# Five engines' hand-written step lists of a cross-attention loop, in another order

## What is computed

```python
q = (hidden_states @ Wq + bq).reshape(b, s, NH, HD).transpose(0, 2, 1, 3)
k = (encoder_hidden_states @ Wk + bk).reshape(b, se, NKV, HD).transpose(0, 2, 1, 3)
v = (encoder_hidden_states @ Wv + bv).reshape(b, se, NKV, HD).transpose(0, 2, 1, 3)
k = jnp.repeat(k, GROUPS, axis=1)
v = jnp.repeat(v, GROUPS, axis=1)
q = _rmsnorm(q, qn_w)
k = _rmsnorm(k, kn_w)
scores = jnp.einsum('bhsd,bhed->bhse', q, k) * scale
scores = scores + attention_mask[:, None, :, :]
probs = jax.nn.softmax(scores.astype(jnp.float32), axis=-1).astype(q.dtype)
out = jnp.einsum('bhse,bhed->bhsd', probs, v)
```

## Time and profile before

| | |
|---|---|
| median of 3 runs | 4682.44 us (4677.71 to 4683.45) |
| profiled execution | 4708.63 us, span 4706.5 us |
| first attention, the 31 rounds from the first score of batch 0 to that of batch 31 | 2221.92 us |
| granted clock of TensorE, mean of the span | 0.911 |

### The profile page before, as it was taken

How to read it: one execution, slowest core, us unless ns; L and a number is a source line. 1 busy time by engine, 2 the same in 40 slices (tenths; PEclk the granted TensorE clock), 3 DMA queues, 4 the chain that set the end, 5 groups by cost and what they waited for, 6 DMA issues and landing times. The chain is left out here.

```text
span 4706.5 us, 104529 instructions
## 1 busy us (share of the span) xinstructions
PE 3904.1 (83%) x34578; PEld 2973.1 (63%) x34579; DVE 3443.8 (73%) x5403; ACT 2449.9 (52%) x4087; POOL 2778.1 (59%) x2145
## 2 busy tenths in 40 slices
PE   5669999999999999999999735883199999999945
PEld 3437777767767776777777724773167767677734
DVE  4657787877877777878877236445789888888957
ACT  4635555545545555555555114331157777777843
POOL 5577777767767776777773144335635555555632
PEclk8879999999999999999999967996599999999966
DMA  6357777767767677687774547554344444444410
GB/s 242 113 133 148 167 153 160 168 132 162 161 141 163 145 159 150 152 173 150 155 160 103 172 127 215 140 141 126 113 123 130 119 123 125 124 118 129 110 38 25
DMA packets 1236097, 657.45 MB, mean 140 GB/s; under 512 B 1087825, under 2 KB 1162449, under 8 KB 1230654
## 3 DMA queue, kind: packets, MB, share of 16 engines
q1 hardware_dynamic: 1218654, 606.60, 54.8%
q0 software_dynamic: 9216, 22.03, 1.6%
q10 hardware_dynamic: 7760, 22.55, 1.3%
HBM read 187.16 MB, written 142.34 MB: 70 GB/s over the span
## 5 line engine op out<-in xcount | busy, mean ns | idle before, releaser
L2007 POOL TENSOR_TENSOR b_pTl<-b_pe,b_pTh 125x1344 f16<-125x1344 f32 x192 | 538.4, 2804 | 482.8 <-ACT b_pTh L2066 458.4
L111 PE MATMUL a_pa<-a_pTh,a_ch 125*128 125x224 f16 x3072 | 796.5, 259 | 1.9 <-DMA a_pTl<-a_pl 1.9
L113 PE MATMUL a_pa<-a_pTh,a_cl 125*128 125x224 f16 x3072 | 795.5, 259 | 0.0
L112 PE MATMUL a_pa<-a_pTl,a_ch 125*128 125x224 f16 x3072 | 795.4, 259 | 0.0
L826 POOL TENSOR_TENSOR a_ksq<-a_kb 125x512 f32<-125x512 f32 x384 | 474.0, 1234 | 350.9 <-DVE a_kb L759 283.4
L698 ACT ACTIVATE a_pr<-a_pr,a_nmax 112x1500 f32<-112x1500 f32 x256 | 395.7, 1546 | 374.3 <-DVE a_nmax L777 374.2
L843 POOL TENSOR_TENSOR a_kb<-a_kb,a_rk 125x512 f32<-125x512 f32 x384 | 540.4, 1407 | 69.1 <-POOL a_kb L843 34.8
L791 DVE SCALAR_TENSOR_TENSOR a_pl<-a_pr,a_inv,a_ph 112x1500 f16<-112x1500 f32 x256 | 502.3, 1962 | 46.1 <-ACT a_ph L705 45.2
L705 ACT ACTIVATE a_ph<-a_pr,a_inv 112x1500 f16<-112x1500 f32 x256 | 395.5, 1545 | 222.1 <-DVE a_inv L786 222.1
L2112 DVE TENSOR_REDUCE b_mx<-b_ps 112x3 f32<-112x1500 f32 x256 | 439.0, 1715 | 95.3 <-PE b_ps L2189 93.9
L777 DVE CUSTOM_DVE_ANT_0 a_pr<-a_ps,a_mask 112x1500 f32<-112x1500 f32 x256 | 438.8, 1714 | 70.3 <-PE a_ps L113 65.3
(11 more groups left out here) (376 smaller groups left out, 10953.5 us busy)
## 6 DMA issues: line engine op xcount, KB each, us to landing
b_ks<-b_kn SPq DMA_DIRECT2D x768, 93.8 KB
scratch_cT<-a_cT SPq DMA_DIRECT2D x64, 768.0 KB
b_cT<-scratch_cT SPq DMA_DIRECT2D x32, 1536.0 KB
a_ctx<-ctx SPq DMA_DIRECT2D x128, 360.0 KB
scratch_xd<-q_zero ACTq DMA_DIRECT2D x4, 4736.0 KB
scratch_yd<-e_y SPq DMA_DIRECT2D x74, 256.0 KB
scratch_oT<-a_ot SPq DMA_DIRECT2D x16, 896.0 KB, 4.2
m_oT<-scratch_oT SPq DMA_DIRECT2D x16, 896.0 KB
```

What stands on the lines that cost most here:

```text
L111: nc.tensor.matmul(out, a_hi, b_hi, start=start, stop=False)
L112: nc.tensor.matmul(out, a_hi, b_lo, start=False, stop=False)
L113: return nc.tensor.matmul(out, a_lo, b_hi, start=False, stop=stop)
L2007: nc.gpsimd.tensor_tensor(pTl[:, n % 2, :, 0:RP], pe_[:, n % NP], pTh[:, n % 2, :, 0:RP], ALU.subtract).then_inc(s["l_pool"], 1)
```

## The change

It reorders the entries of the five lists of `ORDER0`. No instruction is added or removed, and no buffer, shape or wait condition is edited. On TensorE, `P16` moves from the end of a batch's own round to the head of the next (`P16<`), the early `K` move ahead (`K3` before `P17<`, `K5` before `P19<`), the `P` of the round's middle and end come one to two places later relative to `S` and `R`, and the last entries are `O1 P15 R10 R11`. On GpSimd the four `D`, before in two pairs, stand singly: `D1` after `q7`, `D2` after `q9`, `D3` after `N5`, and `D0` after the next batch's `N1` (written `D0>` at the list's end). On SyncE `c1` follows `l0`, `c2` stands ahead of `l2`, `c3` ahead of `l3`, `x0` follows `l5`, `k0` precedes `l7`, `h7` comes after `l7` and `c0>`, and `x1` and `k1` close the list.

```diff
--- before.py
+++ after.py
@@ -404,19 +404,19 @@
 
 ORDER0 = {
     "tensor": """
-        K0 S0 K1 K2 S1 P17< P18< K3 S2 K4 P19< P20< P21< R0 K5 O2< P22< R1 P23< S3 R2 P0 P1 K6 P2 R3 K7 S4 K8
-        P3 P4 R4 S5 P5 K9 S6 R5 P6 P7 P8 R6 K10 O3< P9 P10 K11 S7 P11 R7 R8 P12 P13 O0 P14 P15 R9 P16 R10 R11
-        O1""",
+        P16< K0 S0 K1 K2 S1 K3 P17< P18< S2 K4 K5 P19< P20< R0 O2< P21< R1 P22< P23< S3 K6 R2 P0 P1 R3 K7 S4
+        K8 P2 P3 R4 S5 P4 K9 R5 P5 S6 P6 R6 K10 P7 O3< P8 P9 K11 R7 S7 P10 R8 P11 P12 O0 R9 P13 P14 O1 P15 R10
+        R11""",
     "scalar": """
-        S0 H0 G2< S1 H1 S2 R0 Z2< H2 R1 D0 D1 G3< R2 S3 R3 H3 D2 D3 S4 R4 H4 G0 S5 R5 H5 S6 R6 Z3< H6 G1 R7 S7
-        R8 Z0 H7 R9 R10 R11 Z1""",
+        S0 H0 G2< S1 S2 H1 R0 H2 R1 G3< D0 D1 Z2< R2 S3 R3 H3 S4 R4 H4 D2 S5 R5 H5 S6 R6 Z3< H6 R7 G0 D3 S7 R8
+        G1 Z0 H7 R9 R10 R11 Z1""",
     "vector": """
-        S0 K1 K2 I0 Q0 S1 L0 G2< K3 I1 S2 K4 Q1 L1 I2 R0 Z2< K5 L2 R1 Q2 S3 G3< R2 K6 I3 R3 K7 L3 S4 K8 Q3 I4
-        R4 S5 L4 G0 K9 I5 S6 R5 Q4 L5 I6 R6 Z3< K10 L6 K11 S7 Q5 G1 R7 I7 R8 Z0 L7 R9 R10 R11 Z1 K0>""",
+        Z1< S0 K1 K2 I0 Q0 S1 L0 K3 I1 S2 K4 G2< K5 I2 Q1 L1 R0 Q2 L2 R1 S3 K6 R2 G3< I3 Z2< R3 K7 L3 S4 K8 Q3
+        I4 R4 S5 L4 K9 I5 R5 S6 Q4 L5 I6 R6 Z3< K10 L6 K11 G0 S7 Q5 R7 I7 Z0 R8 G1 R9 L7 R10 R11 K0>""",
     "gpsimd": """
-        D0 D1 N2 q6 q7 D2 D3 q8 N3 q9 N4 q10 q11 N5 q0> q1> q2> N0> q3> q4> N1> q5>""",
+        N2 q6 q7 D1 q8 N3 q9 D2 N4 q10 q11 N5 D3 q0> q1> q2> N0> q3> q4> q5> N1> D0>""",
     "sync": """
-        h0 l0 h1 l1 h2 l2 c2 c3 x0 h3 l3 c0> k0 c1> h4 l4 h5 l5 o0< x1 q0> h6 l6 h7 k1 l7""",
+        h0 l0 c1 h1 l1 c2 l2 h2 h3 c3 l3 h4 q0 l4 h5 l5 o0< x0 h6 l6 k0 l7 c0> h7 x1 k1""",
 }
 ORDER1 = {
     "tensor": """
```

## The result

| | before | after |
|---|---|---|
| median | 4682.94 us (4 runs, 4677.71 to 4686.72) | 4551.6 us (4 runs, 4550.15 to 4552.53) |
| ratio | | 0.9723, 95% interval 0.9711 to 0.9735 |
| profiled execution, span | 4706.5 us | 4550.2 us |
| 31 rounds of the first attention | 2221.9 us | 2086.7 us |
| first reading of batch 0's scores | 312.8 us | 309.8 us |

The change takes 131 us away, a little more than the 115 forecast. The two spans differ by 156 us, of which 137 lie in the attention. The stages behind it are untouched, but TensorE's matmuls of the experts' stage reach over 442 us in the one profiled execution (2773.6 to 3215.4) and over 425 in the other (2637.1 to 3062.0). The profiled execution before lay 26 us above its median and the one after 0.7, so the medians show little of that part.

What follows compares the result with a forecast made beforehand. TensorE bounds the kernel, floor 65.9 us a round; 0.5 (`R9`) and 0.4 (`P6`, seam) make 66.8, saving 94.6 over 31 rounds, plus 21.7 for clock falls, less 1.4 at the end: -115, median 4568, range 4538 to 4660.

Steps and rivals of the forecast that it cites:

- the likeliest case: The forecast itself, both TensorE waits gone: 4538 to 4605 us, time 4568, chance 0.60.
- the 13 falls of the clock: In 13 of 31 rounds the clock falls after the pause before `R11`; all go, 13 x 1.67 = 21.7 us.
- the loop's returns: TensorE's three waits with no releaser, 13.4 us; claimed to cost the same after the change.
- What bounds: TensorE sets the pace: 65.9 us floor in a 69.85 us round, at most 3.95 to be had.
- The signs that were named: Rounds of 66.4 to 67.2 us, VectorE waiting before `Q5` not `Q4`, nearly no clock falls; wrong if a wait exceeds 1.
- The wait before `K11`: TensorE's 1.54 us wait for VectorE's `R6`, late through `q9` behind `D2 D3`; goes with 1.0 to spare.
- The wait before `R11`: TensorE's 1.83 us wait for the last scaling of `N5`; ends at 65.1 against 65.5, so it goes.
- `R9`: `Q5` waits 1.0 for `q11`, so `R7` is taken out at 61.0 against 60.6: 0.5 us wait with handover.
- The seam: Start of a round, `K0` needing `R10`'s bank: with `P16<` and `K0` as cover, costs nothing to 0.5 us.
- `P6` behind `l3`: TensorE's `P6` wants `l3`, issued at 40.6 behind `c3`, at 45.6: wait between nothing and 1.7 us.
- rival A: The wait moves to `P6`, through SyncE's strictly ordered queue with `l3` behind `c3`: 4605 to 4655 us, chance 0.19.
- The lock between GpSimd and VectorE: GpSimd blocked under VectorE's `L`: eight at about 1.2 us a round, 9.6 in all; without it 0.5 a round better.

Runs made afterwards that it cites:

- e10: Kernel before, with only the `D` of GpSimd and ScalarE spread and SyncE's list as in the change; 4619.7 us, ratio 0.9792.
- e5: Changed kernel with GpSimd's four `D` back in two pairs, and ScalarE's `D2 D3` and SyncE's `c3` moved to match; 4676.84 us, ratio 0.999.
- e3: Kernel before, old order, with the power in GpSimd's `N` left out (output no longer correct); 4523.57 us, ratio 0.9659.
- e6: Changed kernel with the end of TensorE's list as before: `K0` first, `P16` ahead of `R10`, `O1` last; 4553.96 us, ratio 0.9726.
- e2: Changed kernel with `h3` also put behind `c3` in SyncE's list; 4575.76 us, ratio 0.9777.
- e7: Changed kernel with the power in GpSimd's `N` left out (output no longer correct); 4512.72 us.

## Why the prediction was right, step by step

The median is 4551.6 against 4568 forecast, in the range of 4538 to 4660 and in that of the likeliest case. In the 31 rounds the forecast saved 94.6 + 21.7 = 116.3; the traces show 135.2. Outside them the 1.4 us more at the end of the last batch came as forecast (62.8 us from its first scores to the last `a_ot` before, 64.4 after), and the first scores come 3.0 us earlier, which the sum did not have. The forecast for the profiled execution, 4594, was off by 42, since that execution had 26 us above its median before and 0.7 after.

| term | forecast | traces |
|---|---|---|
| clean round, 31 times | 69.85 to 66.8: 94.6 | 69.85 to 66.05: 117.8 |
| the 13 falls of the clock | 21.7 | 21.7, no fall left outside the returns |
| the loop's returns, over six rounds | 0 | 37.9 to 32.5: 5.4 |
| late landings of `l3` | in the 66.8 | -5.9, in four rounds (three more are within the returns') |
| ends of the loop and the rest | 0 | -3.8 |

That the gain at the returns, which was not foreseen, makes up for the late landings is chance.

- **What bounds.** TensorE, with the floor of 65.9: right. A clean round stands 0.15 above it. The count of the rounds was off by one: 13 + 11 + 2 + 6 makes 32, and ten rounds, not eleven, have the pause and no fall.
- **The signs that were named.** The mechanism held: no wait of VectorE before `Q4`, 0.53 before `Q5`, no fall of the clock outside the returns. Two signs did not. Clean rounds are below the 66.4 to 67.2. And the prediction called itself wrong if the longest wait of a round is above 1 us anywhere: in rounds 4, 10, 16 and 22 TensorE waits 1.3 to 1.9 for `a_pTl`, so there the cover of `P6` was misjudged, at a price of 5.9 us.
- **The wait before `K11`.** Named rightly, with GpSimd's backlog behind `D2 D3` as its cause; the new ends of `D1`, `q9` and `D2` (39.3, 46.9, 48.8) came within 0.2 of those worked out (39.5, 47.0, 48.9). e10, e5 and e3 show the cause.
- **The wait before `R11`.** It is gone, and the last of `N5` came 0.5 earlier than the sum had it. e10 adds what the argument did not separate: the spread `D` leave 1.1 of it, TensorE's new places of `R10` and `R11` and VectorE's list take the rest.
- **`R9`.** The 0.5 was the largest mis-sized term. `q11` came at 58.7, not 59.2, so `R7` was taken out 0.1 before `R9` wanted the bank. An error of 0.5 in a chain of 59 us was as large as the wait that was read from it. It is 31 x 0.5 = 15.5 us of the forecast's error.
- **The seam.** The sum gave nothing to 0.5, and it is nothing. e6 shows that the cover is used: without `P16<` a clean round waits 0.48. (`O1` was put at 63.8; by the prediction's own units it starts at 63.3, against `G1` at 63.1. It waits for nothing.)
- **`P6` behind `l3`.** The issue was worked out at 40.6 and stands there (1153.86). The thin margin was named; it bites in eight rounds and not in all, 0.3 to 1.9 each, and all but one of them are the first two after the loop's entry or return. 0.4 a round, 12 us, had been laid on it and the seam; outside the returns it cost 5.9. e2 shows what rival A would have been.
- **The clock.** The 13 falls went with the pauses, in the changed kernel and in e3, where only the pauses were taken away.
- **The returns.** "The same cost" was wrong by 5.4. Of these 0.9 lie in the three rounds of the returns and 4.6 in the three after them. The prediction let only the 13 falls in ordinary rounds go; the kernel before has four more in the rounds after the returns, three behind a wait of 2.6 us before `S6` and one behind that before `R11`, and the changed kernel has none there. The round after the first return, before and after, columns as in rows 2:

```profile
953.51:1027.61 74.10, 68.38 (x506) 52.10 (x505) 57.24 (x78) 38.43 (x48) 51.86 (x40) 0.98 0.70 145
...
914.76:984.14 69.38, 64.47 (x495) 50.16 (x496) 56.16 (x80) 37.75 (x48) 51.06 (x40) 1.00 0.67 144
```

  Part of a return's price is what GpSimd has to catch up in the round after it: e7, with GpSimd lighter, shows 65.6 there against 69.3.
- **The lock between GpSimd and VectorE.** It is there as before. The norm of `N4`, 0.20 by itself, takes 1.50 under an `L` (1162.34), and it was right to count it in GpSimd's sum. Over the whole trace of the changed kernel what begins under an `L` ends a fixed time behind it, close to its own full length: squares and scalings (1.04) 0.9 us, a `D` (1.65) or a power (1.64) 1.5, a norm (0.20) 0.05. No run without it was made, so its own price is not measured.

## What to carry to other kernels

When the busiest engine stands still for a short while in each round, follow the wait back to the first engine that was itself waiting for nothing. Here it was one with a busy share of only 75%, whose work stood in an order that served its own pairs and not its customers. Spreading the pieces that nobody waits for at once (the `D`) between those that somebody waits for was worth, with the transfers' order that goes with it, four fifths of the gain in the rounds; the order on the other engines, the busy one among them, was the rest. Then look at the in-order queue of transfers: a transfer that waits for a slow engine must not stand ahead of one that is ready and urgent.

## What the runs showed that was not expected

- **A fall of the clock can be free.** In e5 the granted clock fell in some rounds right after the 2.3 us wait at `R6`. Two neighbouring rounds, columns as in rows 2:

```profile
1168.55:1238.73 70.18, 67.84 (x506) 51.74 (x505) 56.17 (x78) 37.84 (x48) 50.83 (x40) 0.98 0.71 162
1238.73:1309.51 70.78, 66.63 (x506) 51.12 (x505) 55.70 (x78) 38.20 (x48) 52.34 (x40) 1.00 0.73 156
```

  The one with the fall (mean 0.98) is the shorter. There TensorE waits for GpSimd anyway and works the slow stretch off in its own waits: those of 0.38, 0.99 and 0.44 us before `K11`, `R9` and `R11`, shown above for the second round, are not in the first. In the kernel before a fall cost its full 1.67. The same pause of 2.34 is followed by a fall in one round and by none in the next.
- **A return of this loop costs about 11 us**, some 7.5 in its own round (66.05 to 73.5) and 3.3 in the next, and TensorE's own wait at it, 3.4 on average (10.2 in three), is only a third of that. The trace shows where the rest goes in part. A fall of the clock follows TensorE's wait (mean 0.98 in 840.98:914.76). VectorE stands 3.5 to 3.8 at its own return, each time later than TensorE, so the first scores are read some 2.5 us late and TensorE waits 1.7 to 2.0 for it at `S1`. The round after is what a lighter GpSimd takes away (e7). Writing the 32 rounds out took all of it away, 34 us in the median.
